# Decay denominators from TensorE by dt and its square, dt to all partitions by DMA, and another place for one product of the last group

## What is computed

```python
dt    = jnp.clip(softplus(dt_raw + dt_bias), 1e-4, 0.1)     # (T, 4), one per token and head
theta = pi * sigmoid(theta_raw)                              # (4, 128), one per head and state
A     = theta * theta
kdamp = 0.5 * sigmoid(k_raw)                                 # (4, 128)
# each token, for each head and state:
denom = 1.0 + dt * kdamp + dt ** 2 * A
v = (v - dt * A * y + dt * u * Bv) / denom
y = y + dt * v + dt * u * By
```

## Time and profile before

| what | value |
|---|---|
| median of 3 runs (lowest to highest) | 535.52 us (534.62 to 536.36) |
| the profiled execution: its time | 535.58 us |
| the profiled execution: its span in the trace | 533.9 us |
| PE, DVE busy | 439.0 us (82%), 458.2 us (86%) |
| ACT, POOL busy | 256.5 us (48%), 289.9 us (54%) |
| DMA over the span | 7.06 MB, mean 13 GB/s |

### The profile page before, as it was taken

How to read it: one execution, slowest core, us unless ns; L and a number is a source line. 1 busy time by engine, 2 the same in 40 slices (tenths; PEclk the granted TensorE clock), 3 DMA queues, 4 the chain that set the end, 5 groups by cost and what they waited for, 6 DMA issues and landing times.

```text
span 533.9 us, 9649 instructions
## 1 busy us (share of the span) xinstructions
PE 439.0 (82%) x3260; PEld 352.0 (66%) x3260; DVE 458.2 (86%) x1275; ACT 256.5 (48%) x501; POOL 289.9 (54%) x367
## 2 busy tenths in 40 slices
PE   6940159996899969897799969898689969997997
PEld 5830148884757658785666758686556658775986
DVE  6699998979999998979999999988999998788542
ACT  1641127553575526454555626455456534334363
POOL 2027887667108777557306687576405776777000
PEclk9695559999989989999989999999999998999999
DMA  7500000000000001000000000000000000000000
...
DMA packets 8434, 7.06 MB, mean 13 GB/s; under 512 B 1593, under 2 KB 7618, under 8 KB 8258
## 3 DMA queue, kind: packets, MB, share of 16 engines
...
## 4 chain that ended last, share of the span: by engine, by line
DVE 41%; PE 35%; POOL 11%; issue 10%; ACT 3%; DVEq 0%; POOLq 0%; ACTq 0%
PE BC L592 6%; DVE tpA L1287 6%; DVE GV L1287 5%; DVE xr L1435 5%; PE HB L495 4%; DVE BC L1298 4%; PE GV L614 4%; PE HB L552 3%; POOL big L1617 3%; POOL vt L1620 3%; POOL rinv L1655 2%; DVE GV L1298 2%; DVE mm L1335 2%; PE HB L602 2%; PE HB L482 2%
## 5 line engine op out<-in xcount | busy, mean ns | idle before, releaser
L592 PE MATMUL BC<-xnT,winT 128*128 128x128 f32 x512 | 77.3, 299 | 50.4 <-ACT pr L913 29.8
L592 PEld LDWEIGHTS BC<-xnT,winT 128*128 128x128 f32 x512 | 68.0, 207 | 59.9 <-issue 33.4
L1617 POOL TENSOR_TENSOR big<-mm 128x256 f32<-128x256 f32 x64 | 50.1, 782 | 58.3 <-DVE mm L1335 47.4
L1640 POOL TENSOR_SCALAR uT<-uT,skipT 128x512 f32<-128x512 f32 x8 | 17.0, 2136 | 83.4 <-DVE w L1420 53.1
L544 PE MATMUL HB<-xnT,w 128*128 128x512 f32 x108 | 54.9, 637 | 2.3 <-ACT gtm L1000 1.5
L614 PE MATMUL GV<-big,vt 128*128 128x128 f32 x256 | 44.7, 300 | 11.3 <-POOL vt L1620 11.1
L1629 POOL TENSOR_TENSOR mm<-ab,pr 128x256 f32<-128x256 f32 x48 | 41.2, 881 | 18.3 <-ACT pr L913 18.3
L1620 POOL TENSOR_TENSOR vt<-mm 128x256 f32<-128x256 f32 x64 | 49.6, 776 | 0.0
L1333 DVE TENSOR_TENSOR mm<-BC,pr 128x512 f32<-128x512 f32 x64 | 44.2, 690 | 5.7
L614 PEld LDWEIGHTS GV<-big,vt 128*128 128x128 f32 x256 | 35.7, 202 | 20.3 <-POOL vt L1620 17.7
L937 ACT ACTIVATE big<-GV 128x256 f32<-128x256 f32 x60 | 23.0, 383 | 44.3 <-PE GV L617 43.1
...
## 6 DMA issues: line engine op xcount, KB each, us to landing
xr<-in_x SPq DMA_DIRECT2D x4, 256.0 KB, 4.9
...
out<-xr SPq DMA_DIRECT2D x3, 256.0 KB, 2.3
...
```

Of the source, the lines that this page charges most:

```text
L592: last = pe.matmul(b[:, j * TS:(j + 1) * TS], winT[:, col:col + NS], xt, start=True, stop=True)
L1617: pool.tensor_tensor(wt[q % 8][:], m[:, 0], m[:, 3], ALU.add)
```

## The change

Two things are changed.

**Denominators and dt.** DVE writes dt and its square side by side (`dtt`: tile, power, head; one more small multiplication, ordered by the semaphore `dt_sq`). PE turns them with four transposes into 8 rows of 512 tokens, and ACT copies these to `rows8` (first four rows dt, last four dt²; the buffer shares room with `tfs`). A coefficient table `coef8` is made once at the start: PE transposes `kavec` = [kdamp, A], and DVE masks it with `head_mask`, so that `coef8[:, h, :]` holds the two rows of head h and zeros elsewhere. One matmul per head with these 8 rows as weights gives dt·kdamp + dt²·A in PSUM, and ACT takes the logarithm with bias 1 straight from there. L1177, L850, L852 and L862 are gone; so are L840, L1172 and L858 of group 0. For groups 1 to 3, dt reaches `ab` in another way: SP stores the four dt rows to a DRAM tensor `dt_rows`, waits for it, and reads each row back into all 128 partitions with one DMA per head (256 KB each). `beta` now waits for these DMAs (`ld_dt`). In group 0 PE spreads dt with one matmul per head into BC and GV behind the denominators (`first_dt`).

**The last group.** `tail_O` of tiles 12, 13 and 14 is issued right behind `tail_R` of the same tile, not one step later.

```diff
-BCAST_AT, DEN_AT = (9, 10, 12, 13), (11, 12, 14, 14)
+DENS_AT = (9, 10, 12, 13)
...
+        rows8 = tfs[0:2 * NH, 0:GC]
...
+        dt_rows = nc.dram_tensor("dt_rows", (NH, GC), F32, kind="Internal").ap()
...
+            def spread_dt(g):
+                sp.wait_ge(h_free, h_read_of("rows", g))
+                if g > 1:
+                    sp.wait_ge(ld_dt, 16 * NH * (g - 1))
+                sp.dma_start(dt_rows, rows8[0:NH]).then_inc(st_dt, 16)
+                sp.wait_ge(st_dt, 16 * g)
+                sp.wait_ge(fill, FILL_OPS * g)
+                sp.wait_ge(fill_p, POOL_FILL_OPS * g)
+                sp.wait_ge(mat_d, MAT_OPS * g)
+                for h in range(NH):
+                    sp.dma_start(view(ab, DTN + h * SL, (NH * SL, GT), (1, TS)),
+                                 dt_rows[h:h + 1].rearrange("o (c t) -> o c t", c=GT).broadcast_to([128, GT, TS]))\
+                        .then_inc(ld_dt, 16)
             for u, (g, c0, c1) in enumerate(UNITS):
+                if u + 1 < NG:
+                    spread_dt(u + 1)
...
PE, front_early:
-                    pe.transpose(hb[0:KP, 0:TS], dtts[g % 2][:], ident[:]).then_inc(h_ready, 1)
-                    for c in range(GT):
-                        row = NH * c + h
-                        last = pe.matmul(hb[:, c * TS:(c + 1) * TS], ident[0:KP, row:row + 1].broadcast_to([KP, 128]),
-                                         dtr, start=True, stop=True)
+                    for c in range(GT):
+                        last = pe.transpose(hb[0:2 * NH, c * TS:(c + 1) * TS],
+                                            dtts[g % 2][:, c].rearrange("p i h -> p (i h)"), ident[:])
+                    last.then_inc(h_ready, 1)
+                if k in DENS_AT:
+                    h = DENS_AT.index(k)
+                    pe.wait_ge(h_free, h_read_of("rows", g))
+                    hb = h_bank("den", g, h)
+                    pe.matmul(hb[:], coef8[:, h, :], rows8, start=True, stop=True).then_inc(h_ready, 1)
PE, ahead of the loop:
+            pe.wait_ge(prep, 1)
+            pe.transpose(RR[0:2 * NH, 0:NS], kavec[:], ident[:]).then_inc(coef_t, 1)
...
+            for h in range(NH):
+                pe.matmul(DT0[h][:], ident[0:2 * NH, h:h + 1].broadcast_to([2 * NH, 128]), rows8,
+                          start=True, stop=True).then_inc(first_dt, 1)
PE, middle steps:
-                    for tile in due(g, k, TAIL_O):
+                    for tile in due(g, k, TAIL_O) if g < EARLY else ():
                         tail_O(tile)
...
                     for tile in due(g, k, TAIL):
                         tail_R(tile)
+                        if g == EARLY:
+                            tail_O(tile)
ACT, front_early:
-                    act.activation(den_of(h), hb[:].rearrange(...), ACT.Identity,
-                                   bias=kvec[:, h:h + 1], scale=avec[:, h:h + 1])
-                    act.activation(view(ab, DTN + h * SL, (NH * SL, GT), (1, TS)), by_tile(hb[:]), ACT.Copy)\
-                        .then_inc(h_free, 1)
-                if g and k == F_LOG:
-                    act.wait_ge(den_done, NH * (g + 1))
-                    act.activation(lden[:], lden[:], ACT.Ln, bias=1.0).then_inc(ln_den, 1)
+                    act.activation(rows8, hb[0:2 * NH, :], ACT.Copy).then_inc(h_free, 1)
+                    act.activation(den_of(h), hb[:].rearrange("p (c f t) -> p c f t", c=GT, f=2), ACT.Ln, bias=1.0)\
+                        .then_inc(h_free, 1)
DVE:
-                    dve.tensor_scalar(dtts[g % 2][:], lp[0], DT_MIN, DT_MAX, ALU.max, ALU.min).then_inc(dt_done, 1)
+                    dt = dtts[g % 2][:, :, 0, :]
+                    dve.tensor_scalar(dt, lp[0].rearrange("p (c h) -> p c h", c=GT), DT_MIN, DT_MAX, ALU.max, ALU.min)\
+                        .then_inc(dt_sq, 1)
+                    dve.wait_ge(dt_sq, g + 1)
+                    dve.tensor_tensor(dtts[g % 2][:, :, 1, :], dt, dt, ALU.mult).then_inc(dt_done, 1)
...
                 dve.wait_ge(inv_den, NH + g)
+                dve.wait_ge(ld_dt, 16 * NH * g)
...
+            link(dve.tensor_tensor(head_mask[:], ident[0:2 * NH, 0:NH], ident[0:2 * NH, NH:2 * NH], ALU.add))
+            dve.wait_ge(coef_t, 1)
+            for h in range(NH):
+                last = dve.tensor_scalar(coef8[:, h, :], RR[0:2 * NH, 0:NS], head_mask[:, h:h + 1], None, ALU.mult)
+            last.then_inc(coef_done, 1)
```

92 lines of the change are left out of this document (34 added, 58 removed).

## The result

The changed kernel took 533.31 us (median of 11 runs, 531.18 to 535.42) where the kernel before took 535.63 beside it: ratio 0.9963, 95% interval 0.9946 to 0.9979, so 2.3 us faster. A second lot of 12 runs gave 532.03 (ratio 0.9950, 0.9926 to 0.9973). The forecast was 530.2. The sign is right, the time lies in the range, and about half of the forecast gain is missing. The profiled execution, though, took 531.18 (span 529.4), 4.4 us less than the profiled one of before.

A forecast was written before the change was run, and what follows sets the result against it. No engine was taken to bound the whole; PE bounds 222 to 240 us of a round. Terms: −0.7 + 3 × (0.2 − 0.3 − 1.2) − 0.8 = −5.4 from 535.6, so 530.2 us; range 526.0 to 533.6.

The forecast's parts named there:

- Square +0.2: DVE, step 7 of each round: squaring dt adds one small operation and a semaphore, 0.2 us a round, bounds 0.1 and 0.3.
- denominators and logarithm −1.2: Steps 14 to 17 of each round: without this DVE and ACT work, 1.2 us a round saved, bounds 0.6 and 1.8.
- joint −0.3 a round: PE's heads: one 512-column matmul for four of 128 saves 0.1 us at each of three heads, bounds 0 and 0.66.
- POOL's order around the scan: After pair 15: DVE's first scan comes between POOL's two operations and delays the second; second scan 1.2 us earlier.
- the other order: After pair 15: POOL's pair served before DVE's first scan; second scan at 251.5 us, 1.6 us earlier than in the kernel before.
- what can go is the joint of 0.22: PE, each head: four matmuls take 1.08 us, one of 512 columns 0.86; the forecast took half the difference, 0.1.
- DMAs 0: SP's store and four 256 KB reads of dt per round land within a cover of 17 us and cost nothing.
- Start −0.7: Group 0: added work ahead, but fewer steps per head, make the start 0.7 us shorter, bounds 0 and 1.5.
- I count on the clock back at 2.4 GHz for some of them: Group 0: some of the four matmuls spreading dt run at full clock; at low clock 0.6 of 0.9 us is lost.
- Last group −0.8: Early `tail_O` fills PE waits before tiles 12 and 13, tile 14 counted 0; 0.8 us saved, bounds +0.3 and −1.3.
- The terms for tiles 12 and 13, 0.3 and 0.5: Last group: early `tail_O` fills PE waits of 0.29 and 0.73 us before `gv`, worth 0.3 and 0.5 us.
- the same for this purpose: Baseline of the sum: the profiled execution of 535.6 us was used, the median of the runs being 0.1 lower.

The follow-up runs named there:

- e7: The changed kernel with one wait more: DVE's first scan of a round waits until POOL has done both operations of pair 15; 530.01 us, ratio 0.9894.
- e4: The changed kernel with its 8-row matmuls given all 128 rows, the other 120 being zeros; 521.11 us, ratio 0.974.
- e3: The kernel before with only the early `tail_O` of the last group added; 534.64 us, ratio 0.9983.

## Why the prediction was half right

- *Square +0.2, denominators and logarithm −1.2, joint −0.3 a round.* Together −1.3 forecast, −1.2 measured in each round: 1.6 less to pair 15, 0.4 more to the second scan. Counted from dt, the change is 0.2 us behind before at pair 8 (the square) and 0.1 behind at pair 14, so that the heads gave 0.1; from pair 14 to 15 it gains 1.8 and loses 0.4 of it to the second scan, which makes −1.4 for the denominators and the logarithm. POOL's order around the scan was right, and `e7` put a price on the other order.
- *One matmul for four, −0.3.* Failed as a term, and small: 1.05 us against 1.08, so the lower bound, 0, held. The step "what can go is the joint of 0.22" is wrong. The joint is not between the four; it comes from the change of the number of rows: 1.37 and 1.39 us with 8 and 16 rows, 1.08 with 128. The Trainium skill, "TensorE: Matmul & The Clock Gate", section "LDWEIGHTS (loading the stationary operand)", prices a load by its columns. The loads agree (181 to 184 ns for 8 rows, 186 to 192 for 128, at full clock); the conclusion drawn from it, that the joint could go with the number of loads, did not follow. Had the forecast looked at what stands on either side of the 1.08 us it would have found 0.31 ahead of them (226.72 to 227.03), and asked what it was.
- *DMAs 0.* Right, shown by doubling them.
- *Start −0.7.* Between −1.3 and +0.9 from execution to execution. The step "I count on the clock back at 2.4 GHz for some of them" failed: the four matmuls of DT0 all ran at 1.2 GHz, from 20.3 to 27.3 us or 1.74 each (0.86 in `e4`), and the clock came back only when 128-row work had begun. The middle of five starts, −0.5, is near the forecast all the same.
- *Last group −0.8.* Right by chance: −2.0 to pair 15 and +1.2 behind it. The terms for tiles 12 and 13, 0.3 and 0.5, are near the 0.2 and 0.7 of `e3`, and tile 14 at nothing was right. What the sum left out is the last 0.9 us, which DVE gains ahead of pair 15 because it meets POOL at another moment, and the clock, which took back more than half.
- *The frame.* The step that cost the forecast its number is the one that was not priced: the sum against the profiled execution, "the same for this purpose" as the median. That held for before, and the profiled execution of the change lies only 1.0 us above the forecast. But the forecast took over the clock of before for the change, and the change spends 9 us more at 1.2 GHz: outside the stretches that the sum is about, the places where the clock fell took back 2.8 us in one profiled execution and 4.3 in the other. No rival named the clock, although the start's own price (1.64 us a head against 0.86) had shown what it costs.
